# Attention fused with a 1x1 convolution on one core: the score work moved to the head of every attention step

## What is computed

```python
n = h * w                                   # x is (4, 256, 64, 64): n = 4096
q = einsum('oc,bcn->bon', Wq, xf) + bq      # 32 channels
k = einsum('oc,bcn->bon', Wk, xf) + bk      # 32 channels
v = einsum('oc,bcn->bon', Wv, xf) + bv      # 256 channels
att = softmax(einsum('bdi,bdj->bij', q, k) / sqrt(32), axis=-1)   # 4096 x 4096 for each of 4 images
out = gamma * einsum('bcj,bij->bci', v, att)
fused = einsum('oc,bchw->bohw', Wf, concatenate([out, x], axis=1)) + bf
```

## Time and profile before

| | us |
|---|---|
| median of 3 runs | 2155.57 (2155.03 to 2156.54) |
| the profiled execution, its own time | 2154.75 |
| its span | 2152.9 |
| PE busy | 2069.3 (96%) |
| ACT busy | 1740.4 (81%) |
| DVE busy | 1650.1 (77%) |
| POOL busy | 1209.5 (56%) |

### The profile page before, as it was taken

How to read it: one execution, slowest core, us unless ns; L and a number is a source line. 1 busy time by engine, 2 the same in 40 slices (tenths; PEclk the granted TensorE clock), 3 DMA queues, 4 the chain that set the end, 5 groups by cost and what they waited for, 6 DMA issues and landing times.

```text
span 2152.9 us, 45055 instructions
## 1 busy us (share of the span) xinstructions
PE 2069.3 (96%) x16272; PEld 2003.6 (93%) x16272; DVE 1650.1 (77%) x2191; ACT 1740.4 (81%) x2373; POOL 1209.5 (56%) x514
## 2 busy tenths in 40 slices
PE   8899999999989999999998999999999899999999
PEld 7899999999879999999988999999998899999999
DVE  4788888886578888888657888888866788888885
ACT  6788888887678888888777888888877788888886
POOL 0376666677036766666704667666660566676665
PEclk9999999999999999999999999999999999999999
DMA  3200000000320000000031000000003100000000
GB/s 126 82 21 11 19 19 19 19 20 11 105 74 21 21 10 19 19 19 20 11 117 61 21 21 19 10 19 19 20 11 123 35 21 20 19 19 10 19 20 16
DMA packets 54079, 69.44 MB, mean 32 GB/s; under 512 B 4048, under 2 KB 37584, under 8 KB 53968
## 3 DMA queue, kind: packets, MB, share of 16 engines
q1 hardware_dynamic: 53696, 67.91, 9.7%
q10 hardware_dynamic: 272, 0.07, 0.0%
HBM read 34.41 MB, written 33.55 MB: 32 GB/s over the span
## 4 chain that ended last, share of the span: by engine, by line
PE 75%; DVE 12%; issue 9%; ACT 3%; DVEq 0%; DMA 0%; ACTq 0%; SPq 0%
PE ps_o L384 53%; PE ps_s L376 8%; PE ps_p L234 4%; DVE top L612 4%; PE ps_o L234 4%; DVE top L609 3%; ACT raw L456 2%; PE ps_t L234 2%; PE ps_t L276 1%; PE ps_t L268 1%; DVE top_wide L624 1%; DVE top_j L616 1%; PE ps_s L251 1%; DVE top_col L622 1%; DVE raw L629 1%
## 5 line engine op out<-in xcount | busy, mean ns | idle before, releaser
L753 POOL TENSOR_TENSOR raw<-raw,top_m 128x1024 f32<-128x1024 f32 x508 | 1208.8, 2417 | 927.2 <-ACT top_m L461 927.2
L634 DVE TENSOR_TENSOR lo<-ps_p,hi 128x1024 fp32r<-128x1024 f32 x512 | 626.0, 1223 | 334.8 <-ACT ps_p L543 334.8
L384 PE MATMUL ps_o<-val_hi,hi 128*128 128x258 f32 x4096 | 674.5, 287 | 18.2 <-ACT hi L539 18.2
L539 ACT ACTIVATE hi<-raw 128x1024 fp32r<-128x1024 f32 x512 | 544.0, 1062 | 172.4 <-PE ps_o L384 154.2
L384 PE MATMUL ps_o<-val_lo,hi 128*128 128x256 f32 x4096 | 654.7, 282 | 0.0
L612 DVE TENSOR_TENSOR top<-ps_s,top 128x512 f32<-128x512 f32 x896 | 574.1, 682 | 42.0 <-ACT raw L456 41.9
L456 ACT ACTIVATE raw<-ps_s 128x512 f32<-128x512 f32 x1024 | 554.2, 594 | 58.5 <-PE ps_s L376 32.4
L384 PE MATMUL ps_o<-val_hi,lo 128*128 128x258 f32 x4096 | 601.3, 284 | 0.0
L384 PEld LDWEIGHTS ps_o<-val_hi,hi 128*128 128x128 f32 x4096 | 564.4, 190 | 26.2 <-issue 15.0
L384 PEld LDWEIGHTS ps_o<-val_lo,hi 128*128 128x128 f32 x4096 | 563.7, 190 | 0.0
L384 PEld LDWEIGHTS ps_o<-val_hi,lo 128*128 128x128 f32 x4096 | 540.7, 191 | 0.0
(11 more groups left out here) (69 smaller groups left out, 1152.3 us busy)
## 6 DMA issues: line engine op xcount, KB each, us to landing
xf<-x SPq DMA_DIRECT2D x32, 512.0 KB, 3.8
conv_d<-conv_st SPq DMA_DIRECT2D x64, 256.0 KB, 2.1
result<-conv_d SPq DMA_DIRECT2D x64, 256.0 KB, 2.7
out<-result SPq DMA_DIRECT2D x64, 256.0 KB, 2.2
raw<-wf2T SPq DMA_DIRECT2D x1, 256.0 KB, 3.7
raw<-wv SPq DMA_DIRECT2D x1, 256.0 KB, 4.1
raw<-wf1T SPq DMA_DIRECT2D x1, 256.0 KB, 4.4
raw<-wkqT ACTq DMA_DIRECT2D x1, 64.0 KB, 2.1
```

Source lines behind the costliest of these rows:

```text
L384: last = nc.tensor.matmul(ps_o[:, i, 0:width], p[:, t % 2, jl * I + i * P:jl * I + (i + 1) * P], v[:, j, 0:width], start=opens and jl == 0 ...
L539: nc.scalar.activation(hi[:, p], raw[:, slot].rearrange("p j i -> p (j i)"), ACT.Exp, scale=SCALE).then_inc(hi_done, 1)
L634: nc.vector.tensor_tensor(lo[:, t % 2], ps_p[:].rearrange("p h n -> p (h n)"), hi[:, t % 2].bitcast(F32), ALU.subtract).then_inc(lo_done, 1)
L753: nc.gpsimd.tensor_tensor(raw[:, slot], raw[:, slot], top_m[:, r].unsqueeze(1).broadcast_to((P, JQ, I)), ALU.subtract).then_inc(sub_done, 1)
```

## The change

On every engine the score work of a step moves to its head. PE: `scores_ahead(t)` stands before the wait for `hi_done` and before `lead(t, 0)`, in all steps. ACT: `keep_scores` stands before `exponentials(t + 1)`, and has a wait of its own for the full exponential of step t (`p_done`). DVE: `fold_scores` stands before `split_p(t + 1)`; `reduce_top` (t = 4) and `normalise` of half 1 (t = 0) stay ahead of the folds, while `add_conv` (t = 2), `widen_top` (t = 5) and `normalise` of half 0 (t = 7) now come behind the folds of their step. No instruction is added or removed.

```diff
@@ TensorE, attend
                 for t in range(QUADS):
+                    scores_ahead(t)
                     pe.wait_ge(hi_done, Q + (t + 1))
                     lead(t, 0)
-                    if t == 0:
-                        scores_ahead(t)
-                        pe.wait_ge(lo_done, Q + (t + 1))
-                        trail(t, 0)
+                    if 0 < t < QUADS - 1:
                         lead(t, 1)
-                        trail(t, 1)
-                    elif t == QUADS - 1:
-                        pe.wait_ge(lo_done, Q + (t + 1))
-                        trail(t, 0)
-                        scores_ahead(t)
+                    if t == 1 and not first:
+                        pe.wait_ge(m_done, B + 1)
+                        turn_out(B)
+                    if t == 5 and not last_block:
+                        spread_top(B + 1)
+                    pe.wait_ge(lo_done, Q + (t + 1))
+                    trail(t, 0)
+                    if t in (0, QUADS - 1):
                         lead(t, 1)
-                        trail(t, 1)
-                    else:
-                        lead(t, 1)
-                        if t == 1 and not first:
-                            pe.wait_ge(m_done, B + 1)
-                            turn_out(B)
-                        if t == 5 and not last_block:
-                            spread_top(B + 1)
-                        scores_ahead(t)
-                        pe.wait_ge(lo_done, Q + (t + 1))
-                        trail(t, 0)
-                        trail(t, 1)
-                        if t == 4 and not last_block:
-                            turn_top(B + 1, None if first else B)
+                    trail(t, 1)
+                    if t == 4 and not last_block:
+                        turn_top(B + 1, None if first else B)
@@ ScalarE, attend
                 for t in range(QUADS):
+                    if not (isinstance(n, int) and n * QUADS + t + AHEAD >= STEPS):
+
+                        act.wait_ge(p_done, Q + (t + 1))
+                        keep_scores(H, t + AHEAD, 2 * (QUADS * r + t + AHEAD) % BANKS, (QUADS * r + t) % SLOTS)
                     if t < QUADS - 1 or not last_block:
...
                     if t == 5 and not last_block:
                         keep_top(B + 1, (r + 1) % OUTS)
-                    if not (isinstance(n, int) and n * QUADS + t + AHEAD >= STEPS):
-                        keep_scores(H, t + AHEAD, 2 * (QUADS * r + t + AHEAD) % BANKS, (QUADS * r + t) % SLOTS)
@@ VectorE, attend
                     if t == 0 and not first:
                         normalise(B - 1, 1)
+                    if t == 4 and not last_block:
+                        reduce_top(H + 2 * 2 * QUADS)
+                    if not (isinstance(n, int) and n * QUADS + t + AHEAD >= STEPS):
...
+                        fold_scores(H, t + AHEAD, 2 * (QUADS * r + t + AHEAD) % BANKS, old, 0)
                     if t == 2 and not first:
...
                         add_conv(B - 1, before, b * (16 * USES[before]) + (use * 16 + 16))
-                    if t == 4 and not last_block:
-                        reduce_top(H + 2 * 2 * QUADS)
                     if t == 5 and not last_block:
                         widen_top(B + 1)
                     if t == QUADS - 1:
...
                         split_p(Q, t + 1)
...
-                        fold_scores(H, t + AHEAD, 2 * (QUADS * r + t + AHEAD) % BANKS, old, 0)
```

More of the change, by code:

```diff
@@ L719, in attend @@
                         normalise(B - 1, 1)
+                    if t == 4 and not last_block:
+                        reduce_top(H + 2 * 2 * QUADS)
+                    if not (isinstance(n, int) and n * QUADS + t + AHEAD >= STEPS):
+                        q = (t + AHEAD) % QUADS
+                        old = None if q == 0 else 1 if first and t == 0 else 0
+                        if q == 0:
+                            dve.wait_ge(top_j_done, B + 2)
+                        fold_scores(H, t + AHEAD, 2 * (QUADS * r + t + AHEAD) % BANKS, old, 0)
                     if t == 2 and not first:
```

## The result

The changed kernel takes 2195.86 us (median; 2193.78 to 2198.13) against 2155.3 us of before measured beside it, a ratio of 1.0188 with the 95% interval 1.0171 to 1.0206: 40.6 us slower, 1.9%. Forecast were 2191 and +36. The profiled execution took 2194.49 us, its span is 2192.7 us, 39.8 more than before.

The account below looks back on a forecast made before the run. PE bounds the kernel, with one wait a block, of `spread_top` for `top_wide`. The longer chain, 56 x 0.69 = +38.6 us, less 2.4 at image starts, gives +36.2: 2191 us, +1.6%, range 2174 to 2212.

Parts of the forecast that it names:

- What bounds the kernel: PE, busy 2069.3 of 2152.9 us; most of its idle time is `spread_top` waiting for `top_wide`, 55.5 us in 60 times.
- The start of the chain: DVE, step 4: `reduce_top` follows `split_p(4)` and starts 0.75 us after the lead instead of 1.39, a gain of 0.64.
- Its length: DVE, from `reduce_top` to PE's `spread_top`: 6.53 us instead of 5.20, a loss of 1.33.
- The net cost: Each of 56 blocks gets 0.69 us longer, +38.6 us; the wait of `spread_top` grows from 1.0 to 1.8 us.
- Ordinary steps: Scores to scores stay 3.35 us; `lo` has 1.0 us of slack and ACT 0.4; cost 0.
- steps 7 and 0: `lo` some 0.05 us late, lead 1 of step 0 late by 0.16; difference taken as 0, bounds -0.1 and +0.3 a block.
- the extra wait of ScalarE: ACT's new wait for the full exponential is covered by its wait for the scores; without that cover, under 0.1 us.
- POOL: Busy 56%; its maxima come 0.7 us later, against a step-7 use some 5 us on.
- The start of an image: Copies of step 0 come first, so PE's step-1 wait goes: a gain of 0.6 us, four times, -2.4 us.
- The faster rival: Scores ahead of `spread_top` cover its wait, 0.48 us a block: -29 us, 2126; chance 0.07.
- ScalarE holding the scores: Copies' extra wait and DVE's full steps make `lo` 0.3 us late in two steps a block: +36 more, 2227; chance 0.05.
- The fifth rival: A clock that falls behind the longer wait; 1.8 us was held nearer to 1.0 than to 4.5; chance 0.03.

Follow-up runs that it names:

- e9: Changed kernel with `spread_top` on TensorE moved behind the two trails of step 5, VectorE's chain left long; 2140.4 us.
- e10: Changed kernel with one unused VectorE reduction added ahead of `widen_top` and `spread_top` moved behind the trails of step 5; 2203.1 us.
- e1_widen_ahead: Changed kernel with `widen_top` ahead of the folds of step 5 on VectorE instead of behind them; 2127.8 us.
- e5_longer_chain: Changed kernel with one more VectorE reduction, into a tile nobody reads, right ahead of `widen_top`; 2308.5 us.

## Why the prediction was right, point by point

- **What bounds the kernel.** Right: the instruction counts and TensorE's busy time stay (within 7 us), and the change acts through one wait a block. The count of 56 blocks is right too, and e9 and e10 bear it out.
- **The start of the chain.** `reduce_top` was forecast 1.23 us after the scores of step 4; it comes 1035.53 - 1034.33 = 1.20 after, since the folds no longer precede it directly but `split_p(4)` does.
- **Its length.** Forecast 6.53, measured 6.63. The one term that was off is from `reduce_top` to the folds behind it, 2.17 us instead of 2.06; the others (1.21, 1.13, 1.19, 0.45, 0.48) agree within 0.01.
- **The net cost.** `spread_top` comes 7.35 us after lead 0 of step 4 (forecast 7.28, before 6.59), so 0.76 later than before; 0.06 of that comes back elsewhere in the block, where was not traced. A whole block is 0.70 longer (forecast 0.69): 56 x 0.70 = 39.2 of the 39.8 us. The size of the single waits was less well placed: I had 1.8 us in front of `spread_top` (some 105 in all) and 0.2 in front of the scores of step 5, the trace has 1.5 (85.2) and 0.3. My 1.8 did not even take off the 0.2 that I had found in front of it. The scores of step 5 take 1038.79 - 1037.84 = 0.95 us instead of 0.48, and what TensorE loses there it doesn't lose again at `spread_top`.
- **Ordinary steps, steps 7 and 0, the extra wait of ScalarE, POOL.** Costed at nothing, and nothing shows: 1.3 us of waiting for `lo` in the whole span. The distance from scores to scores in steps 2 and 3 is 3.35 us still.
- **The start of an image.** Wrong, -2.4 us. The step that failed is the one that took 3.09 us of ScalarE's idle time as POOL's, because the row names POOL. POOL's subtraction of that quad begins when the maxima are ready, some 8.5 us before ScalarE's start there, and takes 2.4; it had long been done. Nor was it four times: in the kernel before, ScalarE has this idle time at the second and third image only (3.09 and 2.84 us), and the scores wait for the fold at the second alone. In the changed kernel they wait there at the second (0.26 us) and at the third (1.3), and the 56 blocks leave 0.6 us of the 39.8 for everything else. With 38.6 alone the forecast would have been 2194.
- **The faster rival** needed a chain 0.69 us nearer to TensorE to be level with before, and 1.17 for its 0.48 a block. e1_widen_ahead gave 1.2 and its blocks are 0.51 us shorter than before; so the mechanism exists, on the other side of the order of folds and `widen_top`.
- **ScalarE holding the scores** has no wait that speaks for it.
- **The clock.** The fifth rival, a clock that falls behind the longer wait, had chance 0.03 on the ground that 1.8 us is nearer to 1.0 than to 4.5. Behind the 4.54 us wait the kernel before has a granted clock of 0.50 from 622.50 to 625.50 and 1.00 from 626 to 640; the window with the 1.0 us wait has 1.00. In the changed kernel it did not fall at 1.5 us in any block (1.00 in the windows 105:545, 645:1085, 1190:1630 and 1735:2190). But at 2.6 us it does in 33 of the 56 blocks, so the distance to that rival was shorter than the chance suggests: the 1.8 us forecast lie between 1.66, where it never fell, and 2.6, and no run shows that stretch.

## What to carry to other kernels

When an operation stands on a chain that passes through several engines once in a while, look at what each in-order queue puts in front of its links. Moving every engine's frequent work forward also moves it in front of the rare link; here one pair of folds (1.2 us) in front of `widen_top` undid a start that was 0.6 us earlier. Ask first whether the frequent work can stand behind the link, because its own deadline is later: that alone gave 2.7% in the order of before, and 3.1% of the changed kernel's time in the other. And a total that comes out right isn't yet a proof of its terms; compare the terms as well, block by block.

## What the runs showed of the hardware

- The granted clock of TensorE after an idle stretch: it fell in none of 56 blocks after a wait of 1.50 us (after) or 1.66 us (e10_longer_spread_late), where the trace has it at 1.00 throughout; it fell to 0.50, for 3.41 us, in 33 of 56 around a wait of 2.62 us (e5_longer_chain), and those cost 1.43 us more each, with four matmuls in 0.87 us for the 0.48 they take at a granted clock of 1.00. So a wait of 2.6 us cost more than its length here in 33 of 56 blocks; between 1.66 and 2.62 nothing was measured. Behind the wait of 4.54 us in the kernel before the clock was at 0.50 too (622.50 to 625.50).
- A reduction over 1024 elements per partition took 2.04 us from `top` (256 results of four elements that lie 256 apart) and 1.21 us with a broadcast source (128 results of eight). The count of elements alone doesn't give the price.
- On VectorE the next operation started 1.94 us after a `reduce_top` that it doesn't depend on the earlier trace rows and 2.17 us after one whose end it waits for (the copies of step 4, line 601): with the wait on the engine's own last operation it came 0.23 us later. The two following operations differ (a subtraction, a copy), so the wait is the likely cause and not an isolated one.
